# Turning the row maxima of the scores: four 32x32 block transpositions on VectorE in place of a matmul and a copy

## What is computed

```python
def _L0_xattn_ref(Q, K, V, mask, Wq, bq, Wk, bk, Wv, bv, Wo, bo):
    q = (Q @ Wq.T + bq).reshape(b, s, H, DH).transpose(0, 2, 1, 3)
    k = (K @ Wk.T + bk).reshape(b, s, H, DH).transpose(0, 2, 1, 3)
    v = (V @ Wv.T + bv).reshape(b, s, H, DH).transpose(0, 2, 1, 3)
    scores = jnp.einsum('bhqd,bhkd->bhqk', q, k) * SCALE
    scores = jnp.where(mask[:, None, None, :] == 0, -jnp.inf, scores)
    causal = jnp.arange(s)[:, None] >= jnp.arange(s)[None, :]
    scores = jnp.where(causal[None, None], scores, -jnp.inf)
    attn = jax.nn.softmax(scores, axis=-1)
    out = jnp.einsum('bhqk,bhkd->bhqd', attn, v)
    return out.transpose(0, 2, 1, 3).reshape(b, s, d) @ Wo.T + bo

x = x + jnp.tanh(g_xattn[0]) * _L0_xattn_ref(_layernorm(x), ctx_1024, ctx_1024, mask, ...)
# xr, xk: x mixed with the token before it
ffn = sigmoid(xr @ W_r.T) * (square(relu(xk @ W_k.T)) @ W_v.T)
x = x + jnp.tanh(g_ffn[0]) * ffn
```

## Time and profile before

| | |
|---|---|
| median of three runs | 1903.09 us |
| lowest, highest | 1899.09, 1903.93 us |
| profiled execution, span from first to last instruction | 1900.3 us |
| granted TensorE clock, mean | 0.996 |
| busy PE / PEld | 1868.2 us (98%) / 1471.2 us (77%) |
| busy DVE | 1307.8 us (69%) |
| busy ACT / POOL | 1094.9 us (58%) / 1168.8 us (62%) |
| chain that ended last | PE 95%, DVE 3% |
| `max_rows`: matmul L1391, copy L641, DMA L336 | 128 of each |

### The profile page before, as it was taken

One profiled execution on the slowest core, in us unless ns is written; L12 is line 12 of the kernel. 1 busy time (PEld: TensorE's weight loads), 2 busy tenths in 40 slices (PEclk: granted clock), 3 DMA queues, 4 the chain that ended last, 5 costly groups with the idle time before them and its releaser, 6 DMA issues.

```text
span 1900.3 us, 35387 instructions
## 1 busy us (share of the span) xinstructions
PE 1868.2 (98%) x11136; PEld 1471.2 (77%) x11136; DVE 1307.8 (69%) x3680; ACT 1094.9 (58%) x2107; POOL 1168.8 (62%) x1833
## 2 busy tenths in 40 slices
PE   6999999999999999999999999998999999999998
PEld 5677777777777777777777777776778888888887
DVE  6776767776776776767776776777576756657554
ACT  4655555555555655555555555656676656565662
POOL 2776777777777776777777777777543334234331
PEclk9999999999999999999999999998999999999999
DMA  7455465445545455464555545463332231322311
GB/s 219 104 132 127 128 160 125 120 125 138 152 111 141 121 138 131 114 165 119 121 130 132 154 116 135 121 161 100 112 111 89 84 117 67 110 91 77 103 65 67
DMA packets 129226, 229.70 MB, mean 121 GB/s; under 512 B 18800, under 2 KB 20848, under 8 KB 128272
## 3 DMA queue, kind: packets, MB, share of 16 engines
q1 hardware_dynamic: 129040, 227.43, 44.9%
HBM read 92.06 MB, written 33.59 MB: 66 GB/s over the span
## 4 chain that ended last, share of the span: by engine, by line
PE 95%; DVE 3%; issue 1%; DMA 1%; ACT 1%; SPq 0%; ACTq 0%; DVEq 0%
PE proj_ps L41 15%; PE proj_ps L42 15%; PE proj_ps L43 15%; PE score_ps L1382 10%; PE prob_ps L1406 8%; PE value_ps L1425 8%; PE score_ps L41 3%; PE score_ps L42 3%; PE score_ps L43 3%; PE sum_ps L1433 2%; PE sum_ps L41 1%; PE value_ps L41 1%; PE sum_ps L43 1%; PE sum_ps L42 1%; PE value_ps L43 1%; PE value_ps L42 1%
## 5 line engine op out<-in xcount | busy, mean ns | idle before, releaser
L1038 DVE CUSTOM_DVE_ANT_0 score_ps<-score_ps,causal 128x128 f32<-128x128 f32 (+3 forms) x1024 | 488.7, 504 | 291.1 <-PE score_ps L1382 290.9
L654 ACT ACTIVATE probs<-prob_ps 128x512 f32<-128x512 f32 (+1 forms) x768 | 396.0, 528 | 368.9 <-PE prob_ps L1406 184.2
L1382 PE MATMUL score_ps<-k_stack,q_stack 97*128 97x128 f32 (+3 forms) x1024 | 318.8, 352 | 5.5 <-DVE least L1038 4.3
L1406 PE MATMUL prob_ps<-q_stack,k_stack 100*128 100x512 f32 (+3 forms) x1024 | 279.9, 314 | 1.7 <-DMA q_stack<-max_rows 1.5
L459 POOL TENSOR_TENSOR prob_sum<-probs 128x384 f32<-128x384 f32 x256 | 260.1, 1016 | 0.0
L1382 PEld LDWEIGHTS score_ps<-k_stack,q_stack 97*128 97x128 f32 x1024 | 187.3, 189 | 76.2 <-issue 40.9
L527 POOL TENSOR_TENSOR kact<-square,kact 128x512 fp32r<-128x512 f32 x64 | 83.5, 1315 | 236.7 <-ACT kact L737 236.7
L462 POOL TENSOR_TENSOR prob_sum<-prob_sum,probs 128x256 f32<-128x256 f32 x256 | 198.2, 774 | 37.0 <-POOL prob_sum L459 0.4
L1406 PEld LDWEIGHTS prob_ps<-q_stack,k_stack 100*128 100x128 f32 x1024 | 191.7, 190 | 21.1 <-DMA q_stack<-max_rows 2.2
L448 POOL TENSOR_SCALAR_AFFINE_SELECT probs<-probs 128x256 f32<-128x256 f32 x256 | 104.9, 410 | 152.0 <-ACT probs L654 151.8
L452 POOL TENSOR_SCALAR_AFFINE_SELECT probs<-probs 128x256 f32<-128x256 f32 x256 | 106.6, 416 | 126.5 <-ACT probs L654 126.5
(11 more groups left out here) (172 smaller groups left out, 4776.2 us busy)
## 6 DMA issues: line engine op xcount, KB each, us to landing
k_stack<-staged SPq DMA_DIRECT2D x384, 128.0 KB
q_stack<-staged SPq DMA_DIRECT2D x384, 128.0 KB, 3.1
x_io<-in_x SPq DMA_DIRECT2D x16, 1024.0 KB, 7.8
x<-x_io SPq DMA_DIRECT2D x64, 256.0 KB, 3.0
res<-x SPq DMA_DIRECT2D x64, 256.0 KB, 3.6
out_x<-res SPq DMA_DIRECT2D x64, 256.0 KB, 2.0
tiles<-in_x SPq DMA_DIRECT2D x15, 1024.0 KB, 5.5
tiles<-in_ctxT SPq DMA_DIRECT2D x60, 256.0 KB, 4.0
```

The lines of the kernel that those rows point to most:

```text
L654: nc.scalar.activation(probs[:, u % RING, lo:hi], prob_ps[(3 * u + c) % 2][:, 0:hi - lo], ACT.Exp, scale=SCALE).then_inc(exp_done, 1)
L1038: nc.vector.tensor_tensor_reduce(out=here, in0=here, in1=causal[:, LATE - P * t:S], scale=-1.0, scalar=3e38, op0=ALU.add, op1=ALU.min, acc ...
L1382: last = nc.tensor.matmul(here[:, at:at + P * (t + 1)], q_stack[n][0:MASK_ROW + 1, j, P * t:P * t + P], k_stack[n][0:MASK_ROW + 1, j, 0:P ...
L1406: last = nc.tensor.matmul(here[:, at:at + width], k_stack[n][0:ROWS, j, P * k:P * k + P], q_stack[n][0:ROWS, j, P * k:S], start=True, stop ...
```

## The change

VectorE turns the maxima itself. `split_max` becomes 128x32 (its columns 16 to 31 are set to zero once, by POOL), and after the split four `transpose` instructions each turn a block of 32 partitions by 32 columns of it into columns of `max_rows`, now 32x128, whose first 16 rows hold what PE's matmul gave. They wait for the split, and for the DMA that sent the rows of the pair before. PE's matmul, its waits, ACT's copy, the identity in float32r and the wait of PE's sums for the copy go. The DMA has the same size and place in SP's order, and waits for the transpositions.

```diff
-        split_max = sb("split_max", [P, 2 * PAIR * T], F32R)
-        max_rows = sb("max_rows", [2 * PAIR * T, P])
+        split_max = sb("split_max", [P, BLOCK], F32R)
+        max_rows = sb("max_rows", [BLOCK, P])
...
             def stack_maxima(q):
                 n, a = q // 2 % 2, q % 2
-                sp.wait_ge(max_copied, q + 1)
+                sp.wait_ge(max_turned, P // BLOCK * (q + 1))
...
+            nc.gpsimd.memset(split_max[:].bitcast(F32), 0.0).then_inc(max_cleared, 1)
...
-            def copy_maxima(q):
-                act.wait_ge(max_turned, q + 1)
-                if q > 0:
-                    act.wait_ge(max_stacked[(q - 1) // 2 % 2][(q - 1) % 2], 16 * ((q - 1) // 4 + 1))
-                nc.scalar.copy(max_rows[:], sum_ps[0:2 * PAIR * T, 0:P]).then_inc(max_copied, 1)
...
-            nc.scalar.copy(ident_parts[:], ident[:]).then_inc(ident_ready, 1)
...
                 if q > 0:
-                    dve.wait_ge(max_turned, q)
+                    dve.wait_ge(max_turned, P // BLOCK * q)
+                else:
+                    dve.wait_ge(max_cleared, 1)
                 nc.vector.tensor_copy(split_max[:, 0:PAIR * T], here).then_inc(max_high, 1)
                 dve.wait_ge(max_high, q + 1)
                 nc.vector.tensor_tensor(split_max[:, PAIR * T:2 * PAIR * T], here, split_max[:, 0:PAIR * T].bitcast(F32),
                                         ALU.subtract).then_inc(max_split, 1)
+                dve.wait_ge(max_split, q + 1)
+                if q > 0:
+                    dve.wait_ge(max_stacked[(q - 1) // 2 % 2][(q - 1) % 2], 16 * ((q - 1) // 4 + 1))
+                for at in range(0, P, BLOCK):
+                    nc.vector.transpose(max_rows[:, at:at + BLOCK], split_max[at:at + BLOCK, :].bitcast(F32)).then_inc(max_turned, 1)
...
-            def turn_maxima(q):
-                pe.wait_ge(max_split, q + 1)
-                ended = (2 * q + 1 - VALUES) // HG + 1
-                if ended > 0:
-                    pe.wait_ge(refined, ended)
-                nc.tensor.matmul(sum_ps[0:2 * PAIR * T, 0:P], split_max[:], ident_parts[:], start=True, stop=True
-                                 ).then_inc(max_turned, 1)
...
-                pe.wait_ge(max_copied, min(2 * G + 4, N // 2))
...
-                if 2 <= i <= N and i % HG == 0:
-                    turn_maxima(i // 2 - 1)
...
-                if 2 <= i <= N and i % HG == 2:
-                    turn_maxima(i // 2 - 1)
```

More of the change, by code:

```diff
@@ L70, in gated_layer @@
     RING = 5
+    BLOCK = 32
     assert T == 4 and K == 4 and HG == 4 and H == 16
@@ L129, in gated_layer @@
         least = sb("least", [P, 2, PAIR * T])
-        ident_parts = sb("ident_parts", [P, P], F32R)
-        split_max = sb("split_max", [P, 2 * PAIR * T], F32R)
-        max_rows = sb("max_rows", [2 * PAIR * T, P])
+        split_max = sb("split_max", [P, BLOCK], F32R)
+        max_rows = sb("max_rows", [BLOCK, P])
         stats = sb("stats", [P, T, 6])
@@ L157, in gated_layer @@
         mask_loaded, mask_scaled, mask_stored = sem("mask_loaded"), sem("mask_scaled"), sem("mask_stored")
-        ident_ready = sem("ident_ready")
         pool_const, eps_set, stacks_set, bo_ready = sem("pool_const"), sem("eps_set"), sem("stacks_set"), sem("bo_ready")
@@ L176, in gated_layer @@
         scores_done, scores_read = sem("scores_done"), sem("scores_read")
+        max_cleared = sem("max_cleared")
         max_moved, max_high, max_split = sem("max_moved"), sem("max_high"), sem("max_split")
-        max_turned, max_copied = sem("max_turned"), sem("max_copied")
+        max_turned = sem("max_turned")
         max_stacked = [[sem(f"max_stacked{n}_{a}") for a in range(2)] for n in range(2)]
@@ L336, in stack_maxima @@
                 sp.dma_start(q_stack[n][MAX_ROW:MAX_ROW + 2, 2 * a:2 * a + 2, :].bitcast(F32)
-                             .rearrange("r j (t p) -> r (j t) p", p=P), max_rows[:]).then_inc(max_stacked[n][a], 16)
+                             .rearrange("r j (t p) -> r (j t) p", p=P), max_rows[0:2 * PAIR * T]).then_inc(max_stacked[n][a], 16)
             def load_residual(b):
@@ L754, in first @@
                     high_part_attn(K * b)
-                if 2 <= i <= N and i % 2 == 0:
-                    copy_maxima(i // 2 - 1)
             def second(i, b, s):
@@ L893, in _ @@
             split_weights("v", 3)
-            act.wait_ge(pool_const, 5)
-            nc.scalar.copy(ident_parts[:], ident[:]).then_inc(ident_ready, 1)
             act.wait_ge(gate_loaded, 16)
@@ L1627, in _ @@
                     project_v(0, m, k)
-            pe.wait_ge(ident_ready, 1)
             for k in range(2):
```

## The result

| | before | after |
|---|---|---|
| median of four runs | 1903.11 us | 1934.58 us |
| lowest, highest | 1899.09, 1903.93 us | 1933.49, 1936.43 us |
| profiled execution: time, span | not recorded, 1900.3 us | 1933.49 us, 1931.7 us |
| granted TensorE clock, mean | 0.996 | 0.995 |

The ratio after/before is 1.0171, 95% interval 1.0159 to 1.0184: slower. The two medians lie 31.5 us apart, and their quotient, 1.0165, is inside that interval. The forecast was 1924.4 us, +21.3; the range, 1907 to 1940, holds the result, and the size was too small by 10 us.

What follows compares the result with a forecast made beforehand. PE was taken as the bound, with DVE full in some slots: 15 batches at +1.16 (17.4), first batch +3.0, end +0.9, sum +21.3 us, so 1924.4 us for the median; 8-in-10 range 1907 to 1940.

Steps and rivals of the forecast that it cites:

- PE's gain, 0.68 a batch: Removing PE's turning matmuls saves 4 x 0.105 + 4 x 0.065 = 0.68 us a batch, 10.9 us in all.
- The second wait of the transposition is free: The first transposition's wait for the DMA of the pair before costs nothing; that DMA is issued 6.6 us earlier.
- d = 0.91: Delay in us of everything behind the split on DVE; upper bound taken, 0.20 us spacing; lower bound 0.47, worst about 1.3.
- Slot 10, 0.92: PE's output projection load waits for the low part of K: 0.91 + 0.105 - 0.10 spare = 0.92 us stall.
- Slot 6, 0.92: PE's load waits for L1073, no gap in DVE before it: 0.92 us stall; its long 1.30 us left out.
- Slot 2, 0: Third score load has 0.94 us of slack behind the second maximum, even against 0.92, so no stall; slot 14 alike.
- First batch, +3.0: First batch, bound by DVE for a while: four splits at full price, 4 x 0.91 - 0.68 = +3.0 us.
- Last batch and end, 1.16 + 0.9 = 2.06: One of 15 later batches at +1.16 us, plus +0.9 for one split at the end of attention, 1305 to 1325 us.
- rival 1: The transpositions overlap on DVE, delay 0.47 us: +5.8 us, 1909 us; chance 0.15.
- Rival 2: DVE's idle time hides the whole delay and PE's shorter stream makes the kernel faster: 1892 us; chance 0.06.
- Rival 3: The transposition is a slow instruction, delay 1.3 us, slot 2 starting to cost 0.37: +40 us, 1943 us; chance 0.10.
- rival 4: Stalls could make PE's clock lapse in the steady part, some 2 us each; a reason for upward range, no own chance.

Runs made afterwards that it cites:

- experiment 1: Changed kernel without any turning: no transpositions, the DMA sends zero rows, so the maximum is not subtracted; 1891.89 us, ratio 0.9945 to the kernel before.
- experiment 3: Changed kernel with all four transpositions reading partitions 0 to 31, so the maxima of partitions 32 to 127 are left out; 1901.69 us, ratio 0.9996 to before.
- experiment 4: Changed kernel with only two of the four transpositions, partitions 0 to 63, the other maxima left as zeros; 1902.96 us, ratio 1.0005 to before.
- experiment 5: Changed kernel with POOL's four two-input additions replaced by scalings of one tile; 1923.42 us, ratio 1.0115 to before.
- experiment 2: Kernel before, matmul and copy kept, plus four transpositions of a zero tile behind each split, result read by nobody; 1939.92 us, ratio 1.0198 to before.

## Why the prediction came out as it did

- **What bounds the kernel; where the delay lands.** Right for slots 6 and 10: the stalls are where the end of DVE's instruction was 0.05 us ahead of the load, and they come once a batch. Wrong for slot 2, below.
- **PE's gain, 0.68 a batch.** 0.60 measured (experiment 1), 0.08 too high. The slots with products with V gained 0.06 to 0.09 each, the others 0.04 to 0.13. ACT, POOL and SP at nothing: right, the pure removal gives 10.4 us of the 10.9.
- **The second wait of the transposition is free.** Right: in the steady part the trace has none for a DMA.
- **d = 0.91.** 1.04. The upper bound, which I took, was the right kind; the second to fourth transposition and the maximum behind them each start some 0.23 after the one before, not 0.20, which is four times 0.03. The choice of L1050 and L1052 over L1012 as the nearest row is confirmed by experiment 3, which reads like L1012: 0.093.
- **Slot 10, 0.92.** 1.05. My term with the measured d gives 1.04 + 0.105 - 0.10 = 1.045, so only d was off; experiments 3 and 4 fit too (0.53 and 0.58 by the term, 0.49 and 0.59 measured).
- **Slot 6, 0.92.** 0.90, right for two wrong reasons that cancel: d is 0.13 larger, and L1071 is 0.18 shorter. I had seen that 1.30 was "long for its size" and left it out. That was the step that failed, and it failed in experiments 3 and 4 as well, which I priced with the same formula: at d = 0.53 and 0.57 slot 6 cost -0.01 and 0.03.
- **Slot 2, 0.** 0.50 with slot 3. The term compared the second maximum with the third score load, and stopped there. What it left out is farther back, L1073 (now L1071) running into L470: without two-input additions on POOL the stall is 0.23 (experiment 5), so this makes 0.27 of the 0.50. Of the 0.23 the term with the measured d gives 0.10 (1.04 + 0.105 - 0.10 - 0.94); the rest stays open. The longer L1073 was to be worked out from rows of before: L470 began at 442.75, 0.28 after L1073 had ended, and L1073 was to come 0.91 later.
- **First batch, +3.0.** -0.67 + 2.79 = 2.12. **Last batch and end, 1.16 + 0.9 = 2.06.** 2.71.
- **The sum.** Against the forecast: 14 batches at 1.89 for 1.16 are +10.3, the first batch -0.9, the last +0.65, together 10.05 us; by the spans it is 31.35 - 21.3. Of the 0.73 a batch slots 2 and 3 have 0.50, slot 10 has 0.13 and the gain 0.08.
- **The rivals.** Overlap (rival 1) would hold for transpositions of the same partitions, and these are not the same. Its price was too high, though: at d = 0.53 there is no loss. Rival 2 was wrong for the kernel and right for its half: the pairs before slots 4, 8, 12 and 0. Rival 3's d of 1.3 was too high, but its sign, that slot 2 would start to cost, was right. The clock (rival 4) did not lapse from 150 to 1300 us, but it did in the first batch: 0.91 from 40 to 65 us where before had 1.00, in all two lapses of 3.4 us for one. It does not explain that batch's 2.79, though: experiments 2 and 5, with the same d and one lapse there as before, have 3.03 and 2.52.

## What to carry to other kernels

Read which slots of an engine are full, not how busy it is on average: the same instructions cost 31.5 us spread over all slots and gained 3 to 5 us when they stood only where the engine waits. When an instruction is far longer than its like, find what holds it before you shift it by a delay: here its end was tied to another engine's instruction, so in slot 6 a delay of 0.55 us cost nothing, and in slot 2 one of 1.04 put DVE 1.76 late. A saving ahead of a wait is not kept, so gain and cost of a change do not simply add.

## What the runs showed of the hardware

- DVE's 32x32 transpositions in float32 take 0.200 us each by the profile. They start 0.231 us apart when each reads other partitions than the one before, 0.093 when they read the same; one instruction on 128x32 takes 0.212 and turns four blocks.
- A DVE instruction with two SBUF inputs that begins while POOL runs a two-input addition takes the rest of that addition and 0.55 us (60 of 60 before that begin over 0.2 us ahead of its end; 0.74 to 0.75 alone). It goes the other way too: L465 takes 0.46 alone and 0.79 behind L1073, and the pair of L470 grows from 2.54 to 2.98.
- With scalings of one tile on POOL (experiment 5) that wait is hardly seen: 30 of `attn_low` that begin up to 0.38 us ahead of the end of a scaling of `prob_sum` take 0.739 to 0.750, and 16 that begin up to 0.60 ahead of the end of one on 128x384 take 0.740 to 0.746. But the one that begins 1.09 ahead takes 0.967, and the other way round a scaling waits as an addition does: L464 takes 0.53 alone and 0.91 when it begins 0.52 ahead of the end of `attn_low`. The page "SBUF — State Buffer" of the Trainium skill, section "Who interferes with whom", would have any instruction of GpSimd that reads SBUF hold VectorE's. These runs show it for the additions; for the scalings they fit it too if the hold ends some 0.67 us ahead of the recorded end (0.967 = 1.09 - 0.67 + 0.55), and don't decide it.
